# Weights' high and low parts moved to other units of attention, and a rotation's wait split in two

## The reference

```python
h = layernorm(x) * (1 + ca) + sa
x = x + ga * attention(h)              # 32 query heads, 8 key heads, width 64,
                                       # rotary embedding, window of 128 tokens, sinks
h = layernorm(x) * (1 + cb) + sb
h2 = h + attention2(rmsnorm(h))        # 32 query heads, 8 key heads, causal, no rotation
x = x + gb * (h2 + moe(rmsnorm(h2)))   # 8 experts, top 2, relu(up) * gate, down
```

## Time and profile before

| | |
|---|---|
| median of 3 runs | 1041.08 us (1040.23 to 1042.38) |
| the profiled execution | 1044.54 us, span 1043.0 us, mean granted clock 0.962 |
| TensorE busy | 936.6 us, 90% of the span |
| VectorE busy | 749.7 us, 72% |
| ScalarE busy | 754.9 us, 72% |
| GpSimd busy | 521.2 us, 50% |
| HBM read and written | 105.82 MB and 58.79 MB |

### The profile page before, as it was taken

One profiled execution on the slowest core, in us unless ns is written; L12 is line 12 of the kernel. 1 busy time (PEld: TensorE's weight loads), 2 busy tenths in 40 slices (PEclk: granted clock), 3 DMA queues, 4 the chain that ended last, 5 costly groups with the idle time before them and its releaser, 6 DMA issues.

```text
span 1043.0 us, 21616 instructions
## 1 busy us (share of the span) xinstructions
PE 936.6 (90%) x6606; PEld 872.2 (84%) x6606; DVE 749.7 (72%) x2212; ACT 754.9 (72%) x2058; POOL 521.2 (50%) x423
## 2 busy tenths in 40 slices
PE   5679988999888999999999999999998599999991
PEld 3459888888778898989899999999987499999991
DVE  6757886778688776778877777687775766666646
ACT  3358777788768888898888888888886356555540
POOL 5347668777655743644465344333342852222243
PEclk8889999999989999999999999999998699999996
DMA  8789788788447558746565654754303385555324
GB/s 179 184 205 251 216 215 225 199 252 188 121 135 179 152 173 202 193 112 161 133 143 143 163 147 126 171 133 138 96 2 104 122 262 165 170 162 164 102 59 118
DMA packets 146034, 166.02 MB, mean 159 GB/s; under 512 B 79194, under 2 KB 100714, under 8 KB 140800
## 3 DMA queue, kind: packets, MB, share of 16 engines
q1 hardware_dynamic: 129440, 143.58, 53.4%
q0 software_dynamic: 3696, 11.09, 3.4%
q10 hardware_dynamic: 12784, 9.97, 3.1%
HBM read 105.82 MB, written 58.79 MB: 158 GB/s over the span
## 4 chain that ended last, share of the span: by engine, by line
PE 52%; DVE 15%; issue 11%; ACT 11%; POOL 6%; DMA 3%; SPq 0%; ACTq 0%; DVEq 0%; POOLq 0%
PE psO L1112 13%; PE psS L1084 9%; PE psX L1095 8%; PE psP L1013 6%; PE psY L1128 6%; ACT wgt_hi L1342 3%; DVE gated L2096 2%; ACT pbuf L1374 2%; POOL st L826 2%; POOL xg L920 2%; PE psP L1026 2%; DVE pTl L1779 2%; DVE pbuf L1753 1%; DVE pbuf L1756 1%; ACT relu_s L1639 1%
## 5 line engine op out<-in xcount | busy, mean ns | idle before, releaser
L833 POOL TENSOR_TENSOR pbuf<-pbuf,rden 128x768 f32<-128x768 f32 (+3 forms) x128 | 198.3, 1549 | 320.5 <-DVE rden L1774 309.6
L1374 ACT ACTIVATE pbuf<-pbuf,nmax 128x257 f32<-128x257 f32 (+5 forms) x512 | 265.1, 518 | 59.1 <-DVE nmax L1753 52.2
L1084 PE MATMUL psS<-kT,qE 128*128 128x256 f32 (+3 forms) x1024 | 225.8, 313 | 28.7 <-DVE nmax L1753 19.6
L1779 DVE TENSOR_TENSOR pTl<-psX,pTh 128x512 fp32r<-128x512 f32 x272 | 184.8, 687 | 69.9 <-ACT pTh L1342 68.0
L1342 ACT ACTIVATE pTh<-psX 128x512 fp32r<-128x512 f32 x272 | 160.7, 591 | 61.0 <-PE psO L1112 34.6
L1084 PEld LDWEIGHTS psS<-kT,qE 128*128 128x128 f32 x1024 | 159.4, 192 | 42.4 <-DVE nmax L1753 28.2
L1112 PE MATMUL psO<-pTh,vpad 128*128 128x256 f32 x1088 | 186.9, 294 | 3.4 <-DVE ol L1783 3.0
L1095 PE MATMUL psX<-idn,pbuf 128*128 128x128 f32 x1088 | 162.7, 274 | 13.1 <-issue 9.6
L1112 PEld LDWEIGHTS psO<-pTh,vpad 128*128 128x128 f32 x1088 | 149.5, 189 | 11.2 <-DVE ol L1783 6.2
L1095 PEld LDWEIGHTS psX<-idn,pbuf 128*128 128x128 f32 x1088 | 125.1, 141 | 24.2 <-issue 11.6
L1756 DVE CUSTOM_DVE_ANT_0 pbuf<-psS,mcau 128x128 f32<-128x128 f32 (+3 forms) x256 | 123.8, 484 | 19.3 <-PE psS L1084 15.1
(11 more groups left out here) (291 smaller groups left out, 2242.5 us busy)
## 6 DMA issues: line engine op xcount, KB each, us to landing
qd<-st SPq DMA_DIRECT2D x32, 1024.0 KB, 4.5
qE<-qd SPq DMA_DIRECT2D x128, 256.0 KB, 5.8
mrawV<-in_w_moe SPq DMA_DIRECT2D x32, 384.0 KB, 3.6
mrawB<-in_w_moe SPq DMA_DIRECT2D x32, 384.0 KB, 3.4
kT<-kd SPq DMA_DIRECT2D x64, 128.0 KB, 4.3
kT<-kd SPq DMA_DIRECT2D x32, 256.0 KB, 4.7
kd<-st SPq DMA_DIRECT2D x7, 1024.0 KB, 4.8
xg<-sq ACTq DMA_DIRECT2D x7, 640.0 KB, 5.4
```

Source lines behind the costliest of these rows:

```text
L833: G.tensor_tensor(heads, heads, rden[:, u % 4, 0:NORM].unsqueeze(2).broadcast_to([P, NORM, keys(u) * P]), ALU.mult)\
L1084: last = mm(psS[j % 2][:, at:at + n], qE[:, g % 2, j, t * P:(t + 1) * P], kT[:, g % 2, c, k0:k0 + n], start=(c == 0), stop=(c == 1))
L1374: nc.scalar.activation(pj, pj, ACT.Exp, bias=nmax[:, u % 4, j:j + 1], scale=-1.0, accum_out=sums[:, u % 4, j:j + 1]).then_inc(a_exp, 1)
L1779: V.tensor_tensor(pTl[:, kt % 2, :], psX[kt % 2][:, :], pTh[:, kt % 2, :], ALU.subtract).then_inc(v_pl, 1)
```

## The change

In every quad, on ScalarE and GpSimd alike: the part of wq of unit 8 goes to 7 and that of 12 to 13; the part of wo of unit 5 goes to 7 and that of 9 to 10; the part of wkv of unit 2 goes to 1 (that of unit 10 stays). Units 7, 10 and 13 then hold two, and unit 1 too (in quad 0 the wkv alone). On SP load_wq(g + 5) is written in step 5 in place of 6, and load_wo(g + 2) in step 8 behind place(g + 3), in place of step 7 ahead of it (in the windowed steps). VectorE's rotation waits in part 0 for the first of the last rotation's two low parts, and in part 1 for the second, where before part 0 waited for both.

```diff
@@ SP, step_window(u)
-                if m == 6:
+                if m == 5:
                     load_wq(g + 5)
                 if m == 7:
                     store_q(g + 3)
-                    load_wo(g + 2)
                 if m == 8:
                     place(g + 3)
+                    load_wo(g + 2)
@@ GpSimd, low_weights(u); ScalarE, high_weights(u) has the same with high_
-                for at, part in ((0, 3), (4, 4), (8, 5), (12, 6)):
+                for at, part in ((0, 3), (4, 4), (7, 5), (13, 6)):
                     if m == at and 4 * quad + part < NG:
                         low_wq(4 * quad + part)
-                for at, part in ((1, 0), (5, 1), (9, 2), (13, 3)):
+                for at, part in ((1, 0), (7, 1), (10, 2), (13, 3)):
                     if m == at and 4 * quad + part > 0:
                         low_wo(4 * quad + part)
-                if m == 2 and quad + 1 < NQUAD:
+                if m == 1 and quad + 1 < NQUAD:
                     low_wkv(quad + 1, 1)
@@ VectorE, rope(pair, part)
-                    if part == 0:
-                        wait(dve, g_pl, 2 * (TURN[pair] - 1))
+                    wait(dve, g_pl, 2 * (TURN[pair] - 1) - (1 - part))
```

## The result

| | before | after |
|---|---|---|
| median | 1043.06 us (11 runs, 1040.23 to 1045.94) | 1037.21 us (11 runs, 1033.94 to 1040.42) |
| ratio | | 0.9939, 95% interval 0.9922 to 0.9957 |
| the profiled execution | 1044.54 us, span 1043.0 | 1036.73 us, span 1035.2 |
| TensorE busy | 936.6 us | 931.7 us |

The change makes the kernel faster by 5.9 us (4.5 to 8.1 by the interval) where 12.5 were forecast. The median of before is now taken from 11 runs, not three, and lies 2.0 us higher; the move is counted from it.

The account below looks back on a forecast made before the run. TensorE was taken as the bound, with 34 us without a matmul in attention's windowed half to give back. The terms summed to -12.5 us, from the median 1041.1 to 1028.6; range 1021 to 1039.

Parts of the forecast that it names:

- TensorE's stalls: Windowed half: gain counted in TensorE's stalls, not VectorE's waits; -3.2, -5.2, -2.0 us after units 3, 6, 9.
- VectorE's collisions: VectorE's multiply-adds beside GpSimd's low parts: three places freed, two entered; with ScalarE's 1.2 in quad 2, -2.8 us.
- Loads: load_wq and load_wo on the sync queue: both still land in time, wq by 0.5 us; cost 0.
- the slower rival: ScalarE bounds units 7 and 10, its copies waiting for late loads: 24.1 us paid, +7.6, 1049 us; chance 0.06.
- Start: Quad 0, unit 1: wkv's copy delays exponentials and TensorE's transposes; +1.0 us taken, upper bound 2.9.
- Unit 3's slack swallows the delay: Quad 0: unit 3's slack of 2.50 us absorbs the start's delay but is spent; cost 0.2 to 0.3.
- quad 0's own stall after unit 3 stays: Quad 0, after unit 3: TensorE's stall remains, so no gain was counted there.
- Two copies in one unit: ScalarE's second copy in units 7 and 10 of four quads: 0.3 each, +2.4 us; bounds 0 and 9.4.
- The rival in which the pairs cost 0.63 each: Windowed half: 15 pairs at full price, 9.4 us, and the start at 2.9 leave -4.2, 1037 us; chance 0.25.
- Clock: Unit 7 of quads 1 and 2: slow clock after a TensorE stall goes, 1.3 us each, -2.6 us.
- Causal half: Quads 4 on: pairs in unit 7 meet a full ScalarE; +0.6 us taken, bounds -1 and 3.8.
- VectorE's waits did not come back whole: Rival judged: windowed units follow VectorE, so its 14.6 us of waits count and copies stay hidden; 1023 us, chance 0.13.

Follow-up runs that it names:

- e8: The kernel before, unchanged, run again for a second profile: median 1044.18 us, ratio 1.0000.
- e6: The changed kernel with wq's load issued between place_k and place_q, ahead of q's gather: 1032.37 us, ratio 0.9878 to before.
- e4: The changed kernel with the wq part of unit 7 back in unit 8: 1032.00 us, ratio 0.9883 to before.
- e7: The changed kernel with wq back in unit 8, quad 0's wkv in unit 2, the causal half as before: 1030.28 us, ratio 0.9853.
- e9: e7 with quad 0's wkv copy in unit 1 again and its load ahead of q's gather: 1027.04 us, ratio 0.9828 to before.
- e10: The changed kernel with both the wkv and the wq load issued earlier, every copy kept in place: 1029.44 us, ratio 0.9857 to before.
- e1: The kernel before with the wait split alone, every weight in its old unit: 1034.32 us, ratio 0.9904.
- e3: The changed kernel with quad 0's copy of wkv back in unit 2: 1033.47 us, ratio 0.9895 to before.
- e5: The changed kernel with wkv's first load issued ahead of the gather of q, its copy kept in unit 1: 1032.98 us, ratio 0.9894 to before.
- e2: The changed kernel with the old, unsplit wait, so the moves only: 1038.11 us, ratio 0.9941 to before.

## Why the prediction was right and wrong

**Right.** TensorE's stalls were the thing to count: quads 1 to 3 gained 3.9 us in units 3 and 4, where 3.2 were summed. TensorE's stalls at the scores ended at 9.9 (about 9 forecast), line 1715's wait at 0.8, and the units 7 that had the low clock have 1.00. VectorE's collisions moved as written, in both directions. Its pair in quad 0's unit 12 ran 0.95 and 0.48 (before 0.99 and 1.39 in e8), and in unit 13, beside the weights' low parts that GpSimd began at 127.93 and 129.18:

```profile
129.50 1.24 DVE L1685 SCALAR_TENSOR_TENSOR hb<-xN,mv,modb 128x256 f32<-128x256 f32 x1
...
130.78 0.48 DVE L1686 SCALAR_TENSOR_TENSOR hb<-hb,rs,modb 128x256 f32<-128x256 f32 x1
```

It was 0.47 and 0.48, so the price is 0.8 (forecast 0.9), and unit 13 is longer by 0.77. The prediction's worry, that two low parts in a row block one VectorE instruction until the second ends, is not what quad 2's unit 10 shows: there the low parts ended at 283.46 and 284.88, and VectorE's pair at 283.74 and 285.16, one behind each. The three places freed outweigh the entered ones; units 9 to 15 gave 4.2 against 3.6.

**Wrong.** The step that failed is *Loads*: "It fits by 0.5. Cost 0 for both". When the data are needed was right to a tenth; when they land was copied over from before. In quad 1 they landed 2.1 us later against the units, for a margin of 0.5. It cost 3.3 us in units 7 of quads 0 and 1 (e6), and for quad 0 no margin had been worked out at all: there the landing took up to 7.6 us. A cost of 1 us for each late load stood in the text, as a piece of the slower rival, with a chance of 0.06 for it; it should have been a term of its own in the sum, for a margin of 0.5 on three transfers in a row is no margin. (load_wo, the other load moved, is not late in the change: ScalarE waits for woraw once, 1.5 us, before and after alike. But its margin was under 1 us too, and it goes as soon as units 7 are short: ScalarE waits for it in quads 0 and 1 in all five kernels that keep this move and have no wqraw late at unit 7 (e4, e6, e7, e9, e10), for 0.98 and 0.53 us in e6, 1.11 and 0.88 in e10.) The sign that the prediction named for it, ScalarE waiting for wqraw in unit 7, is what the profile showed.

**Start.** The mechanism was right: the copy ahead of the exponentials, TensorE waiting for the scaling, unit 1's denominators at 69.83 (about 69.2 forecast). Its size was not: +1.0 taken, +2.7 measured, near the bound of 2.9. The 69.2 was counted from the end of the copy and came near; but the delay was taken as what lay between it and 67.07, the end of a unit 1 that was 1.5 us long by chance. Against e8 unit 1 is 3.5 us longer, not 2.1. "Unit 3's slack swallows the delay" failed in part, since TensorE came out of a 4.17 us stall with a clock of 0.50, and its queue was longer than the slack; the slow clock named beside it, at 1.3, was real, and 0.9 of it can be read: e4, with the same order of work in these units, takes 5.65 us for unit 3 at 1.00, where the change takes 6.55 at 0.92. Against the profile that was argued from, units 1 to 3 grew by only 0.9 (16.7 to 17.6), because that profile had its own slow unit there. The prediction also did not see that the place is worth something once the load is early, 0.8 to 1.2 us. And "quad 0's own stall after unit 3 stays" was wrong: it was 1.50 us and went with the split, worth 1.2 us in e1 and e3, so against these the move without its data costs 3.8. The late load itself costs 4.7, from the change to e5.

**Two copies in one unit.** 0.3 for each of 8, 2.4, was taken. ScalarE's second copy cost nothing that shows in units 7 of quads 0 and 1; quad 2 paid 0.56 in unit 7 and 0.9 in unit 10, both as collisions on VectorE (in unit 10 that is the collision entered, forecast at 0.2), and quad 3 some 0.3 (5.26 in e6, 4.94 in e4), whose cause is open. The rival in which the pairs cost 0.63 each came out at nearly the measured time (1037), but not for its reason: with the two loads on time and all pairs kept e10 gains 14.9 us by the median. A number that fits does not make its cause right.

**Clock.** 2 x 1.3 was taken. Quad 1's unit 7 did have 1.3 (6.12 to 4.83 in e1 and 4.84 in e6). Quad 2's takes 6.05 us or 6.06 in e1, e4 and e7 without that stall, and 6.04 at a clock of 0.72 before, 6.05 at 1.00 in e8: its length does not follow the clock. VectorE is busy for 5.5 of it, which is probably why. That term should have been 1.3, once.

**Causal half.** +0.6 taken, +1.1 measured; e7 with before's places there has 0.0 to 0.1, so it is the moves: +0.5, +0.9 and +0.5 in units 7 of quads 4, 6 and 7, half or more of it given back in units 8, and +0.9 and +0.5 in units 10 of quads 4 and 6. Quad 5, from which the earlier trace rows were taken, paid nothing (5.57 us after, 5.60 in e8), and quad 7's unit 7 holds one moved copy and no pair. So a busy ScalarE did not tell where the price falls, and the pair alone isn't the cause.

**The rivals.** VectorE's waits did not come back whole: units 3 and 4 of quads 1 to 3 gave 3.9 us, between the 3.2 of TensorE's stalls and the 5.2 of VectorE's waits there. The slower one had the right mechanism, loads that land late, at a third of its price (3.3 and 4.7 us where it had 24.1), without the pairs that were to go with it.

**How near the sum was.** With both loads on time attention gained 11.2 us, 14.3 without the two low-clock units, against 12.5 forecast. Part of that nearness is luck: a clock term of 1.3 too much stands against 1.2 in quad 0's unit 3 and 0.7 in units 3 and 4 of the others that were not counted.

What stays open: units 9 to 15 gained 1.3 us less in e6 and e10 than in the change, most of it in quad 1's unit 9 (-1.0 in place of -1.8). That unit takes 7.20 to 7.25 us in the five kernels in which ScalarE waits for woraw in quad 1, and 6.35 to 6.39 in the change, e3 and e5, in which it doesn't; e1 and e2, with half the change each, have 7.11 and 7.19. So load_wo is the suspect, but no run moved it alone. What makes a causal unit 7 longer by 0.5 or 0.9 is open too.

## What to carry to other kernels

When a step moves earlier on an engine that works in order, its load has to be timed anew in the kernel as it will be: every unit that the change shortens takes slack from a chain of store, gather and load whose own length does not shrink. If the margin comes out below a microsecond, move the load first, and past a gather that waits for its own store; the two such edits were worth 4.4 and 2.5 us in attention here (e5, e6), where the whole change gave 7.4. Then look for the next load in line, as woraw here. And split a wait before moving work to satisfy it: the split alone had 9 of the 15 us, by the medians, that the two together gave with both loads early (e1, e10).

## What the runs showed of the hardware

- The same four weight transfers took 5.8 to 7.6 us from issue to landing behind a gather of q, and 3.7 to 4.3 us ahead of it (quad 0, after and e6).
- A stall of 2.26 us on TensorE ahead of quad 1's unit 7 came with a granted clock of 0.72 in that unit in both profiles of before; with 1.04 us in the same place (e1) the unit had 1.00. But a stall of 2.27 us ahead of quad 2's unit 7 was followed by 0.72 in the first profile and by 1.00 in e8. After TensorE's stalls of 1.6 to 2.1 us ahead of quad 2's unit 0 both happened too: 1.00 in e8 (2.0 us), after (1.6) and e6 (2.0), but 0.80 in e1 (2.1), e9 (1.9) and e10 (1.85), which costs that unit 1.6 us. The length of the stall alone did not decide.
- A VectorE instruction on 128 x 4 elements took 0.72 us in place of 0.17 beside a GpSimd low part (quad 2's unit 7, after and e4).
- Unit 1 of quad 0 ran at 1.00 (4.22 us) or about 0.6 (5.7 us) with the same instructions, in different executions of one kernel (e8 and before).
